# The mixture-of-experts phase: routing weights applied on VectorE, plain paced gathers, and row transpositions in the rounded type

## The chip, the cores and the metric

The kernel runs on one core of a Trainium2 chip. The metric is the device time of one execution in microseconds (us), as the median of several runs; lower is better.

## The reference, cut to what matters

Two decoder layers of attention, cross attention and a feed-forward network, each followed by a layer norm, over 16 x 128 tokens of width 512. The change touches the last network, in which each token goes to the two experts with the highest router scores (8 experts of inner width 352) and to a shared network:

```python
logits = x @ gate_weight.T
scores = jax.nn.softmax(logits, axis=-1)
topk_w, topk_idx = jax.lax.top_k(scores, 2)
combine = jnp.zeros((T, E), x.dtype).at[jnp.arange(T)[:, None], topk_idx].add(topk_w)
gu = jnp.einsum('th,efh->tef', x, gate_up_weights)
act = jax.nn.silu(gu[..., :F]) * gu[..., F:]
y = jnp.einsum('tef,te,ehf->th', act, combine, down_weights)
...
y = y + sact @ shared_down.T
...
x = _layernorm(x + y, axis=-1)
```

## The kernel before

Tokens lie in SBUF as `X`, 128 partitions by 16 token tiles by 512. The program is a row of phases. Each phase gives every engine its own stream of instructions with semaphores between them, written out by hand in the order in which they run. At a phase's end all engines meet at a barrier, clear the phase's semaphores (`Phase.__exit__`, ending at L175) and meet again; nothing of the next phase starts before the slowest engine is through.

Float32 products are made of three products in the rounded type (`float32r`, shown as fp32r): each operand is split into a rounded high part and the rest as a low part, and `products` (L97 to L99) adds high x high, high x low and low x high in PSUM. ScalarE (ACT) writes the high parts, VectorE (DVE) the low ones.

**The shared phase** (function around L1535 to L1900) computes the router, the two expert numbers of each token, their weights `S.score` (token tile t has its lower expert's weight in column t, the higher's in column 16 + t) and the slot of each (token, expert) pair in a list sorted by expert, `S.pos`. Every expert's stretch of slots is filled up to whole tiles of 128: 39 tiles (`TILES`). GpSimd (POOL) scatters the 16 token tiles to both slots in the DRAM tensor `x_slots` (L1624, 32 indirect DMAs), and then the weights to the slots of the DRAM tensor `s_slots`, one float for each partition (L1631, 32 indirect DMAs, a wait for all earlier ones ahead of every second, and a wait for all at the end). Meanwhile TensorE (PE) computes the shared network in loops, and DVE adds its rows to `X` (L1786).

**The expert phase** (`expert_ffn_phase`) runs over the 39 tiles. SP loads a tile of 128 rows of `x_slots` into one of four buffers `xin` (L1967) and its 128 weights into `sc` (L1970). PE transposes the rows in four 128 x 128 pieces (L2146; they are plain float32, against the identity `S.ident`), for tile i + 1 between the up products of tile i and the down products of tile i - 1. ACT and DVE split the result (L2050, L2086), PE makes gate and up (24 products' worth of 352 columns each in three parts), ACT and DVE apply silu and multiply (L2064, L2094), PE transposes the hidden rows (L2191, three pieces), and the down products follow. `store` on ACT copies the result out of PSUM and multiplies it by the row's weight `sc` (L2057); SP stores it to `y_slots` (L1983). POOL splits the next experts' weights (L2008, L2011) and loads the ones after.

**The end of the phase.** When every tile of the experts but the last is stored (`landed`, L2021), POOL issues 16 indirect gathers of the lower expert's rows that the DMA engines add onto `X` (L2035, `compute_op=ALU.add`), one for each token tile and none waiting for another. After the last tile's store has landed it issues 16 plain gathers of the higher expert's rows into `yg`, slices of the two weight staging buffers (L2038; shown as weights_raw and expert_raw). DVE adds each to `X` (L2118), takes the statistics of the row (L2121, L2124), POOL raises to the power -0.5 (L2029), ACT normalizes (L2077) and SP stores the output.

Of the kernel before, what the change touches and what calls it, by code (L numbers as in the profile page):

```python
# [11 lines left out]
P = 128  # L12
# [209 lines left out]
def attention_phase(nc, S, kind, w):  # L222
# [8 lines left out]
    with Phase(nc, kind) as phase:  # L231
# [175 lines left out]
        def _(sp):  # L407
# [30 lines left out]
            if kind == "decay":  # L438
                sp.wait_ge(zero_set, 1)
                with sp.Fori(0, SLOTS // P) as i:  # L440
                    for slots in (S.x_slots, S.y_slots):
                        rows = slots.rearrange("(i p) n -> i p n", p=P)[bass.ds(i, 1)].rearrange("o p n -> (o p) n")
                        sp.dma_start(rows, zeros[:, :]).then_inc(slots_zero, 16)
                sp.dma_start(S.s_slots.rearrange("(p i) n -> p (i n)", p=P), zeros[:, 0:TILES]).then_inc(slots_zero, 16)
                sp.wait_ge(slots_zero, 32 * (SLOTS // P) + 16)
                sp.dma_start(next_c, S.ctx_dram[:, 0:GT, :]).then_inc(next_c_in, 16)
                sp.wait_ge(pp_full, place[("v", G - 1, GT - 1)] + 1)
                sp.wait_ge(s_full, B - GT)
                sp.dma_start(next_q, S.cross["q"].rearrange("p c n -> p (c n)")).then_inc(next_q_in, 16)
                for i, n in enumerate("kv"):  # L450
                    sp.dma_start(next_kv[:, i, :], S.cross[n].rearrange("p c n -> p (c n)")).then_inc(next_kv_in, 16)
# [1065 lines left out]
def shared_ffn_phase(nc, S, w):  # L1517
# [13 lines left out]
    with Phase(nc, "shared") as phase:  # L1531
# [26 lines left out]
        slots_done, rows_done, scattered, scored = sem("slots_done"), sem("rows_done"), sem("scattered"), sem("scored")  # L1558
# [59 lines left out]
        @block.gpsimd  # L1618
        def _(pool):
            pool.wait_ge(slots_done, 1)  # L1620
            for t in range(B):
                for k in range(2):
                    at = bass.IndirectOffsetOnAxis(ap=S.pos[:, k * B + t:k * B + t + 1], axis=0)
                    pool.indirect_dma_start(S.x_slots, at, S.X[:, t, :], None).then_inc(scattered, 16)  # L1624
                if t % GT == GT - 1:
                    pool.wait_ge(scattered, 16 * 2 * (t + 1))
            for n in range(2 * B):
                at = bass.IndirectOffsetOnAxis(ap=S.pos[:, n:n + 1], axis=0)
                if n and n % 2 == 0:
                    pool.wait_ge(scored, 16 * n)  # L1630
                pool.indirect_dma_start(S.s_slots, at, S.score[:, n:n + 1], None).then_inc(scored, 16)  # L1631
            pool.wait_ge(scored, 16 * 2 * B)
# [283 lines left out]
def expert_ffn_phase(nc, S, w):  # L1916
# [8 lines left out]
    with Phase(nc, "expert") as phase:  # L1925
# [4 lines left out]
        xin = sb("xin", [P, NX, DM])  # L1930
# [5 lines left out]
        sc = sb("sc", [P, NX])  # L1936
# [9 lines left out]
        s_in = [sem(f"s_in{b}") for b in range(NX)]  # L1946
        low_added = [sem(f"low_added{b}") for b in range(B)]
        yg_in = [sem(f"yg_in{b}") for b in range(B)]
        high_added = sem("high_added")
        w_hi, w_ready, tile_done, spare_set = sem("w_hi"), sem("w_ready"), sem("tile_done"), sem("spare_set")  # L1950
        tr_full, tr_hi, tr_lo = sem("tr_full"), sem("tr_hi"), sem("tr_lo")
# [13 lines left out]
        def _(sp):  # L1965
            def load(i):
                sp.dma_start(xin[:, i % NX, :], rows(S.x_slots, i)).then_inc(x_in[i % NX], 16)  # L1967

            def load_score(i):
                sp.dma_start(sc[:, i % NX:i % NX + 1], rows(S.s_slots, i)).then_inc(s_in[i % NX], 16)  # L1970
# [3 lines left out]
            for i in range(NX):  # L1974
                load_score(i)
            for e in (1, 2):
                sp.dma_start(raw[e % 2][:, :], w["experts"][e * P:(e + 1) * P, :]).then_inc(first_in[e % 2], 16)
            for i in range(TILES):
# [5 lines left out]
                if i + NX < TILES:  # L1984
                    load_score(i + NX)
# [6 lines left out]
        def _(pool):  # L1992
# [41 lines left out]
            for t in range(B):  # L2034
                pool.indirect_dma_start(S.X[:, t, :], None, S.y_slots, slots(t), compute_op=ALU.add).then_inc(low_added[t], 16)  # L2035
            pool.wait_ge(y_out[(TILES - 1) % 2], 16 * ((TILES - 1) // 2 + 1))
            for t in range(B):
                pool.indirect_dma_start(yg[t], None, S.y_slots, slots(B + t)).then_inc(yg_in[t], 16)  # L2038
                if t >= 9 and t % 4 == 1:
                    norm(t // 4 - 2)  # L2040
# [4 lines left out]
        def _(act):  # L2045
# [6 lines left out]
            def store(i):  # L2052
# [3 lines left out]
                act.wait_ge(s_in[i % NX], 16 * (i // NX + 1))  # L2056
                act.activation(ys[:, i % 2, :], yb[i % 2], ACT.Copy, scale=sc[:, i % NX:i % NX + 1]).then_inc(y_copied, 1)  # L2057

            tokens(0)
# [21 lines left out]
        def _(dve):  # L2081
# [30 lines left out]

            ends = [hi - 1 for lo, hi in sets]
            for n in range(B + 2):
                if n < B:
                    dve.wait_ge(low_added[n], 16)
                    dve.wait_ge(yg_in[n], 16)
                    dve.tensor_tensor(S.X[:, n, :], S.X[:, n, :], yg[n], ALU.add).then_inc(high_added, 1)  # L2118
# [15 lines left out]
        def _(pe):  # L2134
# [5 lines left out]
            def transposes(i):  # L2140
                if i:
                    pe.wait_ge(x_in[i % NX], 16 * (i // NX + (i % NX > 0)))
                    pe.wait_ge(tr_lo, i)
                x = xin[:, i % NX, :] if i else S.first_x
                for c in range(C):
                    m = pe.transpose(tr[:, c * P:(c + 1) * P], x[:, c * P:(c + 1) * P], S.ident[:, :])  # L2146
# [51 lines left out]
def build(nc, a, out, phases=6):  # L2198

    with ExitStack() as ctx:  # L2200
# [19 lines left out]
        S.s_slots = nc.dram_tensor("s_slots", (SLOTS, 1), F32).ap()  # L2220
# [175 lines left out]
```

## Time and profile before

| | us |
|---|---|
| median of 3 runs | 2093.61 (2092.49 to 2094.29) |
| the profiled execution, its own time | 2087.5 |
| its span, first to last instruction | 2085.7 |
| PE busy | 1887.3 (90%) |
| DVE busy | 1041.1 (50%) |
| ACT busy | 713.2 (34%) |
| POOL busy | 385.6 (18%) |
| mean granted TensorE clock | 0.967 |

The span is what lies between the first and the last instruction; the execution's own time is 1.8 us longer. The median of the runs stands 6.1 us above the profiled execution. All positions in the trace (2011.69, say) are us from the start of the span. The granted clock is 1.00 at 2.4 GHz and 0.50 at 1.2 GHz.

### The profile page before, as it was taken

Reading aid. Unit: us, or ns where it says so; the run is one execution under the profiler, and the core shown is the slowest. Engines: PE = TensorE matmul, PEld = TensorE weight load, DVE = VectorE, ACT = ScalarE, POOL = GpSimd, SP = SyncE. Lnnn points to the kernel's source line nnn. Section 1 sums busy time; section 2 is a strip of 40 time slices with the busy share of each in tenths; the row PEclk is TensorE's granted clock in tenths of the full one; section 3 lists DMA queues with packets and bytes.
Section 4 is the critical chain, followed back from the end, with each engine's and each line's share of the span. In section 5 each row is a group of like instructions: output and inputs, shape, how many; then the busy total and the mean of one; then the engine's idle time right before and its main releaser. Section 6 shows DMA issues by size and latency. Waiting matters only on the chain. (4 is left out here: it accounts for less than half of the span.)

```text
span 2085.7 us, 32789 instructions
## 1 busy us (share of the span) xinstructions
PE 1887.3 (90%) x12124; PEld 1535.6 (74%) x12124; DVE 1041.1 (50%) x1836; ACT 713.2 (34%) x2275; POOL 385.6 (18%) x339
## 2 busy tenths in 40 slices
PE   8899888999999989999899998899879995999991
PEld 6667566788888767777677776677658874899990
DVE  5666753455555446333364547677865332222224
ACT  3555624334444332111231102545632210233332
POOL 1111100000000038000021100001104322745335
PEclk9999999999999999999999999999999998999995
DMA  7110142000000022000093000000015100644257
GB/s 238 42 46 14 43 160 82 1 1 1 1 1 1 1 76 91 1 0 0 24 352 115 1 20 27 26 2 1 2 46 207 46 0 0 243 149 143 82 114 205
DMA packets 73375, 135.89 MB, mean 65 GB/s; under 512 B 13456, under 2 KB 31760, under 8 KB 71184
## 3 DMA queue, kind: packets, MB, share of 16 engines
q1 hardware_dynamic: 47376, 96.28, 13.3%
q0 software_dynamic: 7888, 27.94, 4.5%
q10 hardware_dynamic: 17968, 9.71, 1.8%
q8 instruction: 96, 1.57, 0.3%
q14 instruction: 47, 0.39, 0.1%
HBM read 90.62 MB, written 43.29 MB: 64 GB/s over the span
## 5 line engine op out<-in xcount | busy, mean ns | idle before, releaser
L1473 PE MATMUL banks<-ternary_xth,ternary_wq 128*128 (+1 forms) x352 | 140.6, 399 | 5.0 <-DVE ternary_wq L1404 3.6
L1473 PE MATMUL banks<-ternary_xtl,ternary_wq 128*128 (+1 forms) x352 | 139.4, 396 | 0.0
L97 PE MATMUL banks<-latent_vh,latent_cth 128*128 128x512 f32 x256 | 104.2, 407 | 3.5 <-DVE latent_ctl L1174 3.5
L97 PE MATMUL banks<-weights,expert_xgh 128*128 x312 | 104.7, 336 | 2.4 <-DVE expert_xgl L2086 2.4
L99 PE MATMUL banks<-weights,expert_xgl 128*128 x312 | 101.6, 326 | 0.0
L573 ACT ACTIVATE gqa_pr<-banks,gqa_nb 128x128 f32<-128x128 f32 x256 | 90.4, 390 | 32.6 <-DVE gqa_nb L715 32.6
L98 PE MATMUL banks<-weights,expert_xgh 128*128 x312 | 101.4, 325 | 0.0
L573 ACT ACTIVATE causal_pr<-banks,causal_nb 128x128 f32<-128x128 f32 x256 | 90.4, 395 | 31.1 <-DVE causal_nb L715 31.1
L99 PE MATMUL banks<-latent_vh,latent_ctl 128*128 128x512 f32 x256 | 100.1, 391 | 0.0
L98 PE MATMUL banks<-latent_vl,latent_cth 128*128 128x512 f32 x256 | 100.1, 391 | 0.0
L1433 DVE TENSOR_TENSOR ternary_hf<-ternary_sg,banks 128x512 f32<-128x512 f32 x44 | 30.2, 687 | 135.4 <-issue 79.5
L1127 ACT ACTIVATE latent_pt<-banks 128x1024 f32<-128x1024 f32 x32 | 32.9, 1028 | 188.8 <-PE banks L1273 188.8
L1374 ACT ACTIVATE ternary_sg<-banks 128x512 f32<-128x512 f32 x44 | 26.4, 599 | 192.0 <-PE banks L1473 192.0
L1088 POOL TENSOR_TENSOR latent_rs<-latent_ve,mhalf 128x1 f32<-128x1 f32 x15 | 8.2, 550 | 445.6 <-DVE latent_ve L219 445.6
L1118 ACT ACTIVATE latent_pr<-banks,latent_nb 128x128 f32<-128x128 f32 x256 | 90.6, 374 | 0.0
L97 PE MATMUL banks<-latent_xgh,latent_ch 128*128 128x256 f32 x256 | 77.9, 304 | 9.4 <-DVE latent_xgl L1168 4.6
L1473 PEld LDWEIGHTS banks<-ternary_xth,ternary_wq 128*128 128x128 f32 x352 | 67.2, 191 | 23.2 <-DVE ternary_xtl L70 4.3
L1174 DVE TENSOR_TENSOR latent_ctl<-banks,latent_cth 128x512 fp32r<-128x512 f32 x64 | 42.9, 689 | 71.6 <-ACT latent_cth L1105 71.6
L1485 PE MATMUL banks<-ternary_wq,ternary_hh 128*128 128x512 f32 x176 | 70.8, 402 | 8.1 <-DVE ternary_hl L1437 5.8
L1473 PEld LDWEIGHTS banks<-ternary_xtl,ternary_wq 128*128 128x128 f32 x352 | 67.3, 191 | 14.2
L2094 DVE TENSOR_TENSOR expert_hf<-expert_sg,banks 128x352 f32<-128x352 f32 x39 | 20.4, 522 | 105.4 <-PE banks L99 102.9
L98 PE MATMUL banks<-latent_xgl,latent_ch 128*128 128x256 f32 x256 | 72.9, 285 | 0.0
(462 smaller groups left out, 5412.0 us busy)
## 6 DMA issues: line engine op xcount, KB each, us to landing
x_slots<-decay_zeros SPq DMA_DIRECT2D x39, 256.0 KB, 4.3
y_slots<-decay_zeros SPq DMA_DIRECT2D x39, 256.0 KB, 4.5
y_slots<-expert_ys SPq DMA_DIRECT2D x39, 256.0 KB
expert_xin<-x_slots SPq DMA_DIRECT2D x38, 256.0 KB, 2.9
weights_raw<-in_expert_experts SPq DMA_DIRECT2D x4, 2176.0 KB, 9.2
gqa_tw<-in_ternary_w ACTq DMA_DIRECT2D x4, 2112.0 KB
ternary_raw<-in_ternary_w SPq DMA_DIRECT2D x11, 768.0 KB, 4.1
expert_raw<-in_expert_experts POOLq DMA_DIRECT2D x3, 2176.0 KB, 9.7
```

Of the source, the lines that this page charges most:

```text
L97: pe.matmul(out, wh, xh, start=first, stop=False, **kw)
L98: pe.matmul(out, wh, xl, start=False, stop=False, **kw)
L99: return pe.matmul(out, wl, xh, start=False, stop=last, **kw)
L573: a = act.activation(pr[:, h, c, :], S.bank[2 * h + c // 4][:, (c % 4) * P:(c % 4 + 1) * P], ACT.Exp, bias=nb[:, h, c:c + 1], accum_out=su ...
L1118: a = act.activation(pr[:, c, :], S.bank[x][:, j * P:(j + 1) * P], ACT.Exp, bias=nb[:, c:c + 1], accum_out=sums[:, c:c + 1])
L1127: act.activation(pt[:, :, :], pair(1), ACT.Copy).then_inc(pt_done, 1)
L1174: dve.tensor_tensor(ctl[:, x, :], S.bank[2 + x], f32(cth[:, x, :]), ALU.subtract).then_inc(ct_lo, 1)
L1374: act.activation(sg[:, j % 2, :], gate[j % 2][:, :], ACT.Sigmoid).then_inc(sig_done, 1)
L1433: dve.tensor_tensor(hf[:, j % 2, :], sg[:, j % 2, :], up[j % 2][:, :], ALU.mult).then_inc(hf_done, 1)
L1473: a = pe.matmul(dst[:, :], wq[:, j, m, c * P:(c + 1) * P], x[:, c, toks], start=c == 0 and n == 0, stop=c == C - 1 and n == 1)
L1485: a = pe.matmul(yb[i][:, :], h[:, j % 2, i * P:(i + 1) * P], wq[:, j, 2, :], start=j == 0 and n == 0, stop=j == J - 1 and n == 1)
L2094: dve.tensor_tensor(hf[:, i % 2, :], sg[:, i % 2, :], up[i % 2][:, 0:F1], ALU.mult).then_inc(hf_done, 1)
```

## The change

Five things, all for the last network:

- The weights are not scattered to DRAM: the tensor `s_slots`, the DMA that filled it with zeros in an earlier phase, the 32 scatters, the 39 loads of `sc` and their semaphores go. `store` copies without a factor.
- The gathers of the lower expert's rows go into `yg` like the higher's, without an addition. Each from the third on waits until the one two before it has landed.
- DVE gets 16 instructions of a new kind behind its last tile: each multiplies a gathered row by its weight from `S.score` and adds `X`. Its 16 additions of the higher expert's rows become the same kind.
- The gather of the higher expert's rows for token tile t waits until DVE has used the lower rows in the same buffer (`low_added`).
- `xin` is declared in the rounded type, ACT makes a rounded identity `identr` at the phase's start, and the transpositions of tiles 1 to 38 take both and write PSUM in that type. Tile 0 keeps plain float32. The DMA still moves the same bytes into `xin`.

```diff
-                sp.dma_start(S.s_slots.rearrange("(p i) n -> p (i n)", p=P), zeros[:, 0:TILES]).then_inc(slots_zero, 16)
-                sp.wait_ge(slots_zero, 32 * (SLOTS // P) + 16)
+                sp.wait_ge(slots_zero, 32 * (SLOTS // P))
...
-            for n in range(2 * B):
-                at = bass.IndirectOffsetOnAxis(ap=S.pos[:, n:n + 1], axis=0)
-                if n and n % 2 == 0:
-                    pool.wait_ge(scored, 16 * n)
-                pool.indirect_dma_start(S.s_slots, at, S.score[:, n:n + 1], None).then_inc(scored, 16)
-            pool.wait_ge(scored, 16 * 2 * B)
...
-        xin = sb("xin", [P, NX, DM])
+        xin, identr = sb("xin", [P, NX, DM], F32R), sb("identr", [P, P], F32R)
...
-                sp.dma_start(xin[:, i % NX, :], rows(S.x_slots, i)).then_inc(x_in[i % NX], 16)
-
-            def load_score(i):
-                sp.dma_start(sc[:, i % NX:i % NX + 1], rows(S.s_slots, i)).then_inc(s_in[i % NX], 16)
+                sp.dma_start(f32(xin[:, i % NX, :]), rows(S.x_slots, i)).then_inc(x_in[i % NX], 16)
...
             for t in range(B):
-                pool.indirect_dma_start(S.X[:, t, :], None, S.y_slots, slots(t), compute_op=ALU.add).then_inc(low_added[t], 16)
+                if t >= 2:
+                    pool.wait_ge(low_in[t - 2], 16)
+                pool.indirect_dma_start(yg[t], None, S.y_slots, slots(t)).then_inc(low_in[t], 16)
             pool.wait_ge(y_out[(TILES - 1) % 2], 16 * ((TILES - 1) // 2 + 1))
             for t in range(B):
+                pool.wait_ge(low_added, t + 1)
                 pool.indirect_dma_start(yg[t], None, S.y_slots, slots(B + t)).then_inc(yg_in[t], 16)
...
-                act.wait_ge(s_in[i % NX], 16 * (i // NX + 1))
-                act.activation(ys[:, i % 2, :], yb[i % 2], ACT.Copy, scale=sc[:, i % NX:i % NX + 1]).then_inc(y_copied, 1)
+                act.activation(ys[:, i % 2, :], yb[i % 2], ACT.Copy).then_inc(y_copied, 1)
 
+            act.activation(identr[:, :], S.ident[:, :], ACT.Copy).then_inc(ident_rounded, 1)
...
+            def add_scored(n, k):
+
+                x = S.X[:, n, :]
+                return dve.scalar_tensor_tensor(out=x, in0=yg[n], scalar=S.score[:, k * B + n:k * B + n + 1], in1=x,
+                                                op0=ALU.mult, op1=ALU.add)
+
+            for n in range(B):
+                dve.wait_ge(low_in[n], 16)
+                add_scored(n, 0).then_inc(low_added, 1)
...
-                    dve.wait_ge(low_added[n], 16)
                     dve.wait_ge(yg_in[n], 16)
-                    dve.tensor_tensor(S.X[:, n, :], S.X[:, n, :], yg[n], ALU.add).then_inc(high_added, 1)
+                    add_scored(n, 1).then_inc(high_added, 1)
...
                 if i:
+                    pe.wait_ge(ident_rounded, 1)
                     pe.wait_ge(x_in[i % NX], 16 * (i // NX + (i % NX > 0)))
                     pe.wait_ge(tr_lo, i)
-                x = xin[:, i % NX, :] if i else S.first_x
                 for c in range(C):
-                    m = pe.transpose(tr[:, c * P:(c + 1) * P], x[:, c * P:(c + 1) * P], S.ident[:, :])
+                    cols = slice(c * P, (c + 1) * P)
+                    if i:
+                        m = pe.transpose(tr[:, cols].bitcast(F32R), xin[:, i % NX, cols], identr[:, :])
+                    else:
+                        m = pe.transpose(tr[:, cols], S.first_x[:, cols], S.ident[:, :])
```

How it moves instructions on POOL, at the end of the shared phase. Before, from the scatters of rows to the first instruction of the expert phase (L191 to L175 are the barrier and the clearing of the semaphores):

```order
L1624 DMA x_slots<-X,pos 4992x512 x32
L1631 DMA s_slots<-score,pos 4992x1 x32
L1913 UNCONDITIONAL_BRANCH
L191 UNCONDITIONAL_BRANCH
L194 ISA x6
L175 UNCONDITIONAL_BRANCH
L1991 UNCONDITIONAL_BRANCH
L1993 MEMSET expert_spare 128x1
```

With the change:

```order
L1623 DMA x_slots<-X,pos 4992x512 x32
L1906 UNCONDITIONAL_BRANCH
L191 UNCONDITIONAL_BRANCH
L194 ISA x6
L175 UNCONDITIONAL_BRANCH
L1976 UNCONDITIONAL_BRANCH
L1978 MEMSET expert_spare 128x1
```

The 32 scatters of weights were POOL's last work of the phase; now it goes from the scatters of rows straight to the barrier.

POOL at the end of the expert phase. Before:

```order
L2021 TENSOR_TENSOR expert_spare<-expert_spare 128x1
L2035 DMA X<-y_slots,pos 128x512 x16
L2038 DMA weights_raw<-y_slots,pos 128x512 x8
L2038 DMA expert_raw<-y_slots,pos 128x512 x2
L2029 TENSOR_TENSOR expert_rs<-expert_ve,mhalf 128x4
```

With the change:

```order
L2006 TENSOR_TENSOR expert_spare<-expert_spare 128x1
L2022 DMA weights_raw<-y_slots,pos 128x512 x8
L2022 DMA expert_raw<-y_slots,pos 128x512 x8
L2026 DMA weights_raw<-y_slots,pos 128x512 x8
L2026 DMA expert_raw<-y_slots,pos 128x512 x2
L2014 TENSOR_TENSOR expert_rs<-expert_ve,mhalf 128x4
```

The number of gathers is the same and so is their place behind `landed`; the first 16 now fill the buffers that the next 16 fill again.

## Rows read from the trace of the kernel before

**Rows 1.** The page, part 1: engine, busy us, share of the span, instructions.

```profile
PE 1887.3 (90%) x12124; PEld 1535.6 (74%) x12124; DVE 1041.1 (50%) x1836; ACT 713.2 (34%) x2275; POOL 385.6 (18%) x339
```

**Rows 2.** Timeline at this boundary: start us, us, engine, instruction, [idle before <-releaser].

```profile
1749.21 2.74 DVE L1786 TENSOR_TENSOR X<-X,banks 128x512 f32 x4 [1.17 <-PE banks L99]
...
1750.72 0.39 PE L99 MATMUL banks<-weights,shared_hl 64*128 64x512 f32 x1
...
1759.55 0.96 POOL L1631 DMA_INDIRECT s_slots<-score,pos  x1 [0.30 <-issue]
...
1771.95 0.10 POOL L1993 MEMSET expert_spare<- 128x1 f32 x1 [11.44 <-POOLq L175]
...
1771.99 1.09 PE L2146 MATMUL banks<-ident,first_x 128*128 128x128 f32 x4 [20.88 <-PEq L175]
```

**Rows 3.** Waits from 1650 us on: total us, times, longest.

```profile
POOL s_slots L1631 <- DMA s_slots<-score,pos: 78.0, 13, 7.4
```

**Rows 4.** Timeline at three other phase boundaries.

```profile
1530.99 0.55 DVE L624 TENSOR_SCALAR X<-X,causal_mv,causal_rs 128x512 f32<-128x512 f32 x1 [0.66 <-POOL causal_rs L483]
1533.47 2.79 PE L60 MATMUL banks<-ident,X 128*128 128x128 f32 x12 [5.12 <-PEq L175]
...
1037.40 1.94 PE L809 MATMUL banks<-ident,X 128*128 128x128 f32 x16 [2.81 <-PEq L175]
...
272.06 1.94 PE L1213 MATMUL banks<-ident,X 128*128 128x128 f32 x8 [2.76 <-PEq L175]
```

**Rows 5.** Stretches: us, busy PE, PEld, DVE, ACT, POOL, then granted clock, DMA share, GB/s.

```profile
1752.50:1753.00 0.50, 0.00 (x0) 0.00 (x0) 0.00 (x0) 0.00 (x0) 0.10 (x1) 0.91 0.00 0
...
1780.00:1781.00 1.00, 1.00 (x8) 1.00 (x7) 0.00 (x0) 0.00 (x0) 0.00 (x0) 0.89 0.85 366
...
272.00:274.00 2.00, 1.94 (x10) 1.98 (x10) 0.19 (x1) 0.60 (x1) 0.00 (x0) 0.50 0.42 91
...
1037.00:1039.00 2.00, 1.60 (x15) 1.63 (x16) 0.00 (x0) 0.00 (x0) 0.53 (x1) 1.00 0.29 90
```

**Rows 6.** The chain that ended last, expert phase: start us, us on it.

```profile
1778.57 0.29 PE banks L97
...
1784.09 0.16 PE banks L97
...
1887.72 0.44 PE banks L2146 x4
...
1894.39 0.44 PE banks L2146 x4
```

**Rows 7.** Groups by line and shape: busy us, mean ns of one.

```profile
L98 PEld LDWEIGHTS banks<-weights,expert_xgh 128*128 128x128 f32 x312 | 59.7, 191 | 0.0
...
L2146 PEld LDWEIGHTS banks<-ident,expert_xin 128*128 128x128 f32 x152 | 18.9, 140 | 0.8
...
L1404 DVE SCALAR_TENSOR_TENSOR ternary_wq<-ternary_raw,ternary_thr,ternary_below 128x512 fp32r<-128x512 f32 x33 | 25.7, 825 | 2.8 <-POOL ternary_below L1355 2.8
```

**Rows 8.** Timeline of the end of the expert phase.

```profile
2011.69 1.69 POOL L2035 DMA_INDIRECT X<-y_slots,pos  x1 [0.15 <-issue]
...
2037.97 0.56 DVE L2100 TENSOR_TENSOR expert_htl<-banks,expert_hth 128x384 fp32r<-128x384 f32 x1 [2.61 <-ACT expert_hth L2072]
...
2039.50 1.54 POOL L2035 DMA_INDIRECT X<-y_slots,pos  x1 [0.31 <-issue]
...
2042.00 0.69 ACT L2057 ACTIVATE expert_ys<-banks,expert_sc 128x512 f32<-128x512 f32 x1 [4.06 <-PE banks L99]
...
2046.16 0.99 POOL L2038 DMA_INDIRECT weights_raw<-y_slots,pos  x1 [5.12 <-DMA y_slots<-expert_ys]
...
2049.54 0.69 DVE L2118 TENSOR_TENSOR X<-X,weights_raw 128x512 f32<-128x512 f32 x1 [11.01 <-DMA weights_raw<-y_slots,pos]
```

**Rows 9.** DMA issues from 1650 us on: median us from issue to landing.

```profile
X<-y_slots,pos POOLq DMA_INDIRECT x16, 5.8
weights_raw<-y_slots,pos POOLq DMA_INDIRECT x8, 3.6
```

More of the change, by code:

```diff
@@ L1557, in shared_ffn_phase @@
         route_in, given_done, ranked = sem("route_in"), sem("given_done"), sem("ranked")
-        slots_done, rows_done, scattered, scored = sem("slots_done"), sem("rows_done"), sem("scattered"), sem("scored")
+        slots_done, rows_done, scattered = sem("slots_done"), sem("rows_done"), sem("scattered")
         gw_in, gw_zero, first_x_in = sem("gw_in"), sem("gw_zero"), sem("first_x_in")
@@ L1935, in expert_ffn_phase @@
         ys = sb("ys", [P, 2, DM])
-        sc = sb("sc", [P, NX])
         six, mv = sb("six", [P, B, 6]), sb("mv", [P, B, 2])
@@ L1945, in expert_ffn_phase @@
         y_out = [sem(f"y_out{b}") for b in range(2)]
-        s_in = [sem(f"s_in{b}") for b in range(NX)]
-        low_added = [sem(f"low_added{b}") for b in range(B)]
+        low_in = [sem(f"low_in{b}") for b in range(B)]
         yg_in = [sem(f"yg_in{b}") for b in range(B)]
-        high_added = sem("high_added")
+        low_added, high_added = sem("low_added"), sem("high_added")
         w_hi, w_ready, tile_done, spare_set = sem("w_hi"), sem("w_ready"), sem("tile_done"), sem("spare_set")
+        ident_rounded = sem("ident_rounded")
         tr_full, tr_hi, tr_lo = sem("tr_full"), sem("tr_hi"), sem("tr_lo")
@@ L1966, in load @@
             def load(i):
-                sp.dma_start(xin[:, i % NX, :], rows(S.x_slots, i)).then_inc(x_in[i % NX], 16)
-            def load_score(i):
-                sp.dma_start(sc[:, i % NX:i % NX + 1], rows(S.s_slots, i)).then_inc(s_in[i % NX], 16)
+                sp.dma_start(f32(xin[:, i % NX, :]), rows(S.x_slots, i)).then_inc(x_in[i % NX], 16)
             for i in range(1, NX):
                 load(i)
-            for i in range(NX):
-                load_score(i)
             for e in (1, 2):
@@ L1983, in _ @@
                 sp.dma_start(rows(S.y_slots, i), ys[:, i % 2, :]).then_inc(y_out[i % 2], 16)
-                if i + NX < TILES:
-                    load_score(i + NX)
             for t in range(B):
@@ L2219, in build @@
         S.landed_at = sb("landed_at", [P, E], U32)
-        S.s_slots = nc.dram_tensor("s_slots", (SLOTS, 1), F32).ap()
         S.ring, S.owner1 = sb("ring", [P, TILES], U32), sb("owner1", [P, TILES], U32)
```

## The prediction

> **What bounds the kernel now.** I read the busy shares first: PE works 90% of the span [rows 1], so only what PE executes, or what holds PE up, is worth much. The list of waits and the timeline around the start of the expert phase come next, since the change takes work out there. PE's last product before the barrier starts at 1750.72 and is over by 1751.11; DVE's last addition to `X` ends at 1749.21 + 2.74 = 1751.95; but the next phase starts only at 1771.95, after PE has stood idle for 20.88 us [rows 2]. POOL is what is late: its last scatter of weights is issued until 1759.55 + 0.96 = 1760.51 and then it waits 11.44 us for the landing and the barrier [rows 2]. It got so late because every second scatter waits for the ones before, 78.0 us over 13 waits, 6.0 us each [rows 3]. The third view is the chain that ended last, in the 39 tiles: it is PE's without a gap, a tile each 1894.39 - 1887.72 = 6.67 us, the four transpositions on it with 0.44 us [rows 6]. Of this stage only PE's own instructions count. The last view is the timeline behind the tiles: the store of the last tile (ACT at 2042.00, landed at 2046.16) and then POOL's 16 gathers, with DVE behind each [rows 8].
>
> **The change part by part.** The sum is made against the profiled execution's own 2087.5 us and then moved to the median of the runs, which stands 6.1 us higher (2093.6).
>
> (1) The 32 scatters of weights go. POOL's last work of the phase is then the scatters of rows, done long before, and DVE's addition that ends at 1751.95 becomes the last. What a barrier costs behind the last worker is shown by the boundary before: DVE ends at 1530.99 + 0.55 = 1531.54 and PE starts at 1533.47, 1.93 us [rows 4]. So the expert phase starts at 1751.95 + 1.93 = 1753.9 instead of 1772.0: **18.1 us**. All of it is on the path: PE waits from 1751.11 to the new phase and then runs without a gap. Next late would be DVE, whose addition waits for PE itself.
>
> (2) The clock after the shorter gap. Now PE restarts at the half clock: the four first transpositions take 1.09 us [rows 2] against 0.44, and 19 products take 0.29 us instead of 0.16 [rows 6] until the clock is back shortly after 1780 [rows 5]: 0.65 + 19 x 0.13 = 3.1 us lost. With the change PE is idle from 1751.11 to 1753.9, 2.8 us. Two earlier gaps of that length (2.81 and 2.76 us, [rows 4]) ended one at 1.00 and one at 0.50 [rows 5]. Here the clock had fallen by 1753 (0.91 over the half microsecond from 1752.50 [rows 5]), ahead of the new start, so the start is likely at the half clock again, with a return possibly sooner. Bounds 0 and 3.1; I take **1.0 us** gained.
>
> (3) The loads of weights and the zero fill. SP's 39 small loads go, of which the first four stand ahead of the two big weight loads. Nobody waits for those on PE: the chain in the tiles holds PE only. 0 us; covered by PE. The same for ACT's factor: a copy on ACT beside PE, 0 us apart from the last tile's. ACT's rounding of the identity stands ahead of its first copy, under the first transpositions: 0.
>
> (4) The transpositions of 38 tiles, 152 instructions, now cost 0.44 / 4 = 0.110 us each on the chain [rows 6]. No transposition and no product of under 256 columns in the rounded type is in the trace, so the new price is bounded. Below: a rounded product of 352 columns takes 0.16 us [rows 6], 147 ns of it at 2.4 columns a ns; 128 columns would be 53 ns, at most 14 ns more, and I take 53 as the end: 152 x 57 ns = 8.7 us gained. Above: the weight load of a rounded product takes 191 ns against 140 ns in a transposition [rows 7]; if the new form loads its weights the slow way, the 51 ns more stand where the stream saves, and nothing is gained, or it is even dearer (a rival below). The two rows pull apart equally and no row is nearer, so I take the middle, 85 ns: 152 x 25 ns = **3.8 us** gained, ends 0 and 8.7. The rule that speaks against this part: by the Trainium skill, "TensorE: Matmul & The Clock Gate", Terms (the row on the xbus), TRN2 has a transpose mode that is four times faster for float32. By that rule plain float32 rows already have the fast way and the retyping gives 0; that is the second rival below.
>
> (5) The gathers of the lower rows. Before, they start at 2011.69 and the last is issued until 2039.50 + 1.54 = 2041.04, 1.84 us apart [rows 8]; POOL then has 5.1 us of slack until the last store has landed at 2046.16. Now each is a plain gather, 0.99 us of issue, and two are in flight. A plain gather lands in 3.6 us, one with addition in 5.8 [rows 9]. With some 0.3 us to wake up, a pair takes 3.9 us, 1.95 each: 16 x 1.95 = 31.2 us, until 2042.9. That is still 3.3 us ahead of 2046.16, so 0 us; stores and row loads that run beside it may eat that margin, hence up to 2 us of loss in the range. The break-even is (2046.16 - 2011.69) / 16 = 2.15 us each.
>
> (6) DVE's new instructions. 16 multiply-adds begin once DVE has finished the last tile at 2037.97 + 0.56 = 2038.53 [rows 8]. The nearest price is an addition of the same size, 0.69 us [rows 8]; the only multiply-add of 512 columns in the trace takes 0.825 us [rows 7], with another output type. 16 x 0.69 = 11.0 us ends at 2049.6, when DVE is first wanted for a higher row (2049.54): hidden. By 0.825 it would end 2.2 us late and the 16 in the tail would each be 0.14 us longer, some 2 us in all. I take 0. POOL's added wait for `low_added` before each higher gather is met early: DVE works at 0.7 us a row from 2038.5, POOL issues at 1.3 us a row from 2046.
>
> (7) The last store. ACT's copy at 2042.00 starts 1 us after PE has ended and its buffer's previous store was still under way beside the adding gathers; the last store itself needs until 2046.16. With fewer transfers beside them I expect **1.0 us** less, bounds 0 and 1.6.
>
> Sum: 18.1 + 1.0 + 3.8 + 1.0 = 23.9 us. 2087.5 - 23.9 = 2063.6 for the profiled kind of execution, 2093.6 - 23.9 = **2069.7 us** for the median.
>
> **The rivals.**
>
> The retyping gives nothing: the rounded rows take 110 ns as before. For it speaks that the trace's transposition and plain product look alike and the slow weight load; against it the rounded stream. 2069.7 + 3.8 = 2073.5 us.
>
> The rounded type is dear when narrow: every rounded product here is at least 256 wide. If a 128-wide one went at the plain product's four passes, 4 x 53 = 213 ns, it would cost 152 x 103 ns = 15.7 us more than now: 2093.6 - 20.1 + 15.7 = 2089.2 us.
>
> The lower gathers are late because a gather beside the tiles' traffic takes 5.8 us, as the adding ones do now [rows 9]: a pair each 6.1 us, 16 x 3.05 = 48.8 us against the 34.5 there are, 14.3 us late: 2084.0 us. Against it: the adding ones read and write `X`, and the plain ones in the tail need 3.6 us.
>
> Slower than before: the same pacing, two at a time, makes the weights' scatters stand 6.0 us per pair in waits on top of 2.5 us of issue [rows 2, 3], 8.5 us a pair. If the lower gathers went like that, 16 x 4.25 = 68 us, the first higher gather would be 33.5 us late: 2103.2 us. It decides from 28 us of lateness on, (34.5 + 28) / 16 = 3.9 us a gather. Against it: those scatters write 4 bytes to each slot in DRAM, the gathers whole rows into SBUF.
>
> **How the numbers follow.** My forecast 0.48, the retyping gives nothing 0.29, dear when narrow 0.10, gathers at 5.8 us 0.09, gathers like the scatters 0.04. The forecast with all its ends spans 18.1 + 3.1 + 8.7 + 1.6 = 31.5 gained (2062) to 18.1 alone with 4 us lost in (5) and (6) (2079.5); that includes the first rival and leaves out the other three, some 0.2. A difference under 0.2% (4.2 us) can't be told from none here. Faster by more: the first two, gathers at 5.8 us, and half of the narrow case, whose 2089.2 lies at the bound (2089.4): 0.91. Within: 0.05. Slower: 0.04.
>
> **What would show it.** The gap of PE at the start of the expert phase shrinks from 20.9 to about 2.8 us and POOL has no indirect DMA behind the scatters of rows. The granted clock around the new start tells (2). The four transpositions on the chain take 0.34 us a tile if (4) holds, 0.44 if not, 0.85 if narrow is dear. POOL's lower gathers stand 1.8 to 2.1 us apart; if over 2.15, the first higher gather starts later than the last store's landing. DVE's multiply-adds show 0.69 or 0.83 us. The prediction is wrong if the gap stays above 5 us, or if the stretch from ACT's last copy to the end (43.7 us now, from 2042.00) grows.

## The result and the profile after

The median fell from 2093.12 us (2092.49 to 2094.29, 4 runs of each) to 2067.73 us (2067.34 to 2068.66): a ratio of 0.9881, 95% interval 0.9866 to 0.9897. The forecast was 2069.7 us, range 2062.0 to 2079.5. The profiled execution of the changed kernel took 2068.66 us, its span 2066.9 us.

The page of the changed kernel, part 1, answers to [rows 1]; POOL has 32 instructions and 39 us less:

```profile
PE 1886.0 (91%) x12124; PEld 1533.9 (74%) x12124; DVE 1052.3 (51%) x1852; ACT 708.4 (34%) x2276; POOL 346.9 (17%) x307
```

The timeline at the start of the expert phase, to be held against [rows 2]:

```profile
1749.13 2.76 DVE L1779 TENSOR_TENSOR X<-X,banks 128x512 f32 x4 [1.18 <-PE banks L99]
...
1750.66 0.39 PE L99 MATMUL banks<-weights,shared_hl 64*128 64x512 f32 x1
...
1753.09 0.10 POOL L1978 MEMSET expert_spare<- 128x1 f32 x1 [125.94 <-POOLq L175]
...
1753.13 1.09 PE L2147 MATMUL banks<-ident,first_x 128*128 128x128 f32 x4 [2.08 <-PEq L175]
```

POOL is now idle for 125.94 us until the expert phase starts, and PE stands for 2.08 us instead of 20.88. The tile loop on the chain that ended last, answering to [rows 6], with the products around the transpositions; first the changed kernel:

```profile
1866.73 0.16 PE banks L99
1866.89 0.30 PE banks L2145 x4
1867.19 0.30 PE banks L97
1867.49 0.23 PE banks L98
```

and the same place in the kernel before:

```profile
1887.56 0.16 PE banks L99
1887.72 0.44 PE banks L2146 x4
1888.15 0.23 PE banks L97
1888.39 0.23 PE banks L98
```

The four transpositions take 0.14 us less, and the first product behind them 0.07 us more. The timeline of the end, answering to [rows 8]:

```profile
1989.51 1.05 POOL L2022 DMA_INDIRECT weights_raw<-y_slots,pos  x1 [0.15 <-issue]
...
2016.06 5.38 DVE L2104 SCALAR_TENSOR_TENSOR X<-weights_raw,score,X 128x512 f32<-128x512 f32 x8
...
2018.66 0.60 ACT L2044 ACTIVATE expert_ys<-banks 128x512 f32<-128x512 f32 x1 [3.11 <-PE banks L99]
2019.51 1.42 POOL L2022 DMA_INDIRECT expert_raw<-y_slots,pos  x1 [0.57 <-DVE X L2104]
2021.36 5.38 DVE L2104 SCALAR_TENSOR_TENSOR X<-expert_raw,score,X 128x512 f32<-128x512 f32 x8
2022.39 5.17 POOL L2026 DMA_INDIRECT weights_raw<-y_slots,pos  x1 [1.46 <-DMA y_slots<-expert_ys]
2027.86 0.95 POOL L2026 DMA_INDIRECT weights_raw<-y_slots,pos  x1 [0.30 <-issue]
...
2029.94 0.75 DVE L2104 SCALAR_TENSOR_TENSOR X<-weights_raw,score,X 128x512 f32<-128x512 f32 x1 [3.20 <-DMA weights_raw<-y_slots,pos]
```

One row was not foreseen in the prediction: the first higher gather takes 5.17 us to issue, where it took 0.99 [rows 8]. In the same time DVE does its second eight multiply-adds.

So the span, 2085.7 to 2066.9 us, splits into four stretches without remainder:

| stretch | before | after | gained |
|---|---|---|---|
| span start to first transposition of the expert phase | 1771.99 | 1753.13 | 18.9 |
| from there to the end of PE's last product | 269.0 | 265.5 | 3.5 |
| from there to the first higher gather | 5.2 | 3.8 | 1.4 |
| first higher gather to the end | 39.5 | 44.5 | -5.0 |

The traces give 18.8 us, the medians 25.4 us. Of the 6.6 us between them, 5.6 are on the side of the kernel before, whose profiled execution lay that far under its median (2087.5 and 2093.12); the other 1.0 is the changed kernel's, whose profiled execution was its slowest (2068.66 against 2067.73). In the runs below, which stand beside 8 to 15 runs of the kernel before, that one has a median of 2082 to 2084 us, and the gain is 18.5 us. Why it stood near 2093 in the first measurement stays open.

### The profile page after: what moved, and what is told of

The parts are those of the page before. It is cut to its first block and busy times, and to the rows that moved or that the text cites. A ratio compares the mean times of both kernels' runs of the same rounds, so it can differ in the third digit from the quotient of the medians.

```text
span 2066.9 us, 32715 instructions
## 1 busy us (share of the span) xinstructions
PE 1886.0 (91%) x12124; PEld 1533.9 (74%) x12124; DVE 1052.3 (51%) x1852; ACT 708.4 (34%) x2276; POOL 346.9 (17%) x307
```

## The experiments

Positions in the table come from each run's profile: start of the expert phase (first transposition), the stretch of PE from there to the end of its last product, the issue time of the first higher gather, and the stretch from that gather to the end. The ratio is to runs of the kernel before that were timed beside it, with its 95% interval. The runs were made on four different chips, so across them only the ratios can be compared. The first group (r_before_again, r_round_only, r_after_again, r_plain_transposes) ran on one chip.

| run | median us | ratio | start | PE stretch | issue | to the end |
|---|---|---|---|---|---|---|
| r_before_again | 2084.16 (one) | | 1769.0 | 267.9 | 0.99 | 39.8 |
| r_no_scatter | 2064.91 | 0.9918 (0.9904 to 0.9932) | 1749.6 | 268.3 | 0.99 | 40.0 |
| r_round_only | 2082.37 | 0.9993 (0.9984 to 1.0002) | 1768.8 | 266.2 | 0.99 | 40.2 |
| r_after_again | 2065.21 | 0.9905 (0.989 to 0.992) | 1751.2 | 265.0 | 5.41 | 44.2 |
| r_plain_transposes | 2067.4 | 0.992 (0.9906 to 0.9933) | 1752.2 | 268.3 | 6.01 | 44.4 |
| r_low_narrow | 2059.69 | 0.9889 (0.987 to 0.9909) | 1751.1 | 265.2 | 0.95 | 39.5 |
| r_low_gap | 2062.72 | 0.9907 (0.9887 to 0.9926) | 1751.0 | 265.4 | 1.32 | 40.9 |
| r_low_split | 2063.01 | 0.9906 (0.9887 to 0.9925) | 1750.2 | 265.0 | 0.95 | 42.4 |
| r_gap_late | 2062.78 | 0.9908 (0.9893 to 0.9923) | 1752.8 | 265.3 | 0.96 | 40.1 |
| r_no_pace | 2080.28 | 0.9992 (0.9982 to 1.0002) | 1749.8 | 280.3 | 5.51 | 44.8 |
| r_pace4 | 2080.12 | 0.9994 (0.9984 to 1.0003) | 1750.5 | 280.4 | 5.49 | 44.4 |
| r_pace3 | 2067.26 | 0.9936 (0.9914 to 0.9959) | 1749.0 | 268.1 | 5.40 | 44.3 |

**Both kernels again.**

> The kernel before, unchanged, for a second trace of it. Theory A (the profiled execution of before was a quick one because its paced scatters of weights happened to land quickly): POOL's last scatter and so the start of the expert phase stand at another place, by 3 to 8 us later than 1772.0, with the row scatters, the tile period (6.67) and the tail as they were. Theory B (the 6 us between its time and the median lie anywhere else): the start of the expert phase is within 1 us of 1772.0.

> The changed kernel, unchanged, timed beside the others and traced a second time. Theory A (DVE's back-to-back multiply-adds hold off POOL's writing of the first higher gather until they are through): that gather's issue takes 4 to 6 us again and ends within 1 us of the end of the 16th multiply-add. Theory B (the 5.17 us were an accident of that execution): it takes 1.0 to 1.5 us and the tail from its start to the end is 40 us instead of 44.5.

For the kernel before neither theory holds: the expert phase starts at 1769.04, 3.0 us sooner than in the first trace, and not 3 to 8 us later or within 1 us. So the scatters had not landed unusually early in the first trace, and they don't explain the 6 us. For the changed kernel theory A holds: the issue takes 5.41 us and ends 0.83 us behind the 16th multiply-add.

The change is 18.5 us here by the medians (2083.74 of the 15 runs of the kernel before, 2065.21) and by the spans (2082.4, 2063.9). The parts are much the same as in the first pair: 17.9 at the start, 3.0 in PE's stretch, 2.1 ahead of the first higher gather, -4.4 behind it.

**The scatters alone taken out of the kernel before.** This run leaves out the routing weights, since nothing writes them to the slots.

```diff
-            for n in range(2 * B):
-                at = bass.IndirectOffsetOnAxis(ap=S.pos[:, n:n + 1], axis=0)
-                if n and n % 2 == 0:
-                    pool.wait_ge(scored, 16 * n)
-                pool.indirect_dma_start(S.s_slots, at, S.score[:, n:n + 1], None).then_inc(scored, 16)
-            pool.wait_ge(scored, 16 * 2 * B)
```

> The kernel before without its 32 scatters of the routing weights (it leaves out the weights: the tiles' factors are read as the zeros that the slots hold). All else as before, the 39 small loads of factors and the adding gathers too. Theory A (the scatters are the whole of the gain and the new end of the phase is a loss): the expert phase starts at about 1751 to 1753, 18 us earlier, the tail stays as before, and the kernel is 18 to 20 us faster than before, so as fast as the changed kernel with plain transpositions or up to 3 us faster. Theory B (the plain gathers bring a part of the gain): it is 2 us or more slower than that kernel.

Its median is 16.9 us under that of the kernel before, its span 19.2 us under r_before_again's, all of it at the start (1769.0 to 1749.6). The scatters by themselves make up the whole gain of the change as the repeated runs show it, within the intervals (0.9918 against r_after_again's 0.9905); the other four edits come to about nothing together. Only the first measurement, 0.9881 with its slow kernel before, lies outside. The next runs take that nothing apart.

**The rounded transpositions, alone and left out.** Once as the only edit to the kernel before (r_round_only), once the changed kernel without it (r_plain_transposes, whose edit this is):

```diff
                 for c in range(C):
                     cols = slice(c * P, (c + 1) * P)
-                    if i:
-                        m = pe.transpose(tr[:, cols].bitcast(F32R), xin[:, i % NX, cols], identr[:, :])
-                    else:
-                        m = pe.transpose(tr[:, cols], S.first_x[:, cols], S.ident[:, :])
+                    x = f32(xin[:, i % NX, cols]) if i else S.first_x[:, cols]
+                    m = pe.transpose(tr[:, cols], x, S.ident[:, :])
```

> The kernel before with nothing but the rounded transpositions. Theory A: 2.4 us faster than before, tile period 6.61, the gap ahead of the expert phase unchanged at some 20 us. Theory B: 5.6 us faster. Theory C: no change.

> The changed kernel with its 152 row transpositions in plain float32 against the plain identity. Theory A (the trace's reading: a rounded transposition is 37 ns shorter, but the product behind it grows from 0.23 to 0.30 us because its weight load is no longer covered, so the retyping gives 0.06 us a tile): 2.4 us slower than the changed kernel, tile period 6.67. Theory B (the retyping is worth its full 0.15 us a tile): 5.6 us slower than the changed kernel. Theory C (worth nothing): the same time as the changed kernel within 0.7 us.

ACT's silu, one in each tile, shows the period without PE's modelled ends. From the timelines of ACT, two tiles that lie 26 apart, in r_plain_transposes:

```profile
1798.43 0.46 ACT L2052 ACTIVATE expert_sg<-banks 128x352 f32<-128x352 f32 x1 [1.28 <-PE banks L99]
...
1972.28 0.46 ACT L2052 ACTIVATE expert_sg<-banks 128x352 f32<-128x352 f32 x1 [1.28 <-PE banks L99]
```

and in r_after_again:

```profile
1803.43 0.47 ACT L2052 ACTIVATE expert_sg<-banks 128x352 f32<-128x352 f32 x1 [0.70 <-PE banks L99]
...
1975.12 0.47 ACT L2052 ACTIVATE expert_sg<-banks 128x352 f32<-128x352 f32 x1 [1.27 <-PE banks L99]
```

173.85 / 26 = 6.687 us against 171.69 / 26 = 6.603 us: 0.08 us a tile, 38 x 0.08 = 3.0 us. In the kernel before the same two places give 6.683, in r_round_only 6.603. PE's stretch agrees in sign: 3.3 us shorter with the rounded form in the changed kernel, 1.8 us in the kernel before. In the latter pair the clock adds its own share: it was back 5.75 us after the start in r_before_again and 8.75 us in r_round_only. The medians (2.2 us between the two changed ones, 0.9993 for the edit alone) agree, but couldn't have told it from nothing.

**DVE's multiply-adds beside POOL's first higher gather.** Three ways to take DVE out of POOL's way. r_low_narrow cuts the lower multiply-adds to 2 of 512 columns and so leaves most of the lower expert's rows out of the sum:

```diff
-            def add_scored(n, k):
+            def add_scored(n, k, w=DM):
...
-                x = S.X[:, n, :]
-                return dve.scalar_tensor_tensor(out=x, in0=yg[n],
+                x = S.X[:, n, 0:w]
+                return dve.scalar_tensor_tensor(out=x, in0=yg[n][:, 0:w],
...
-                add_scored(n, 0).then_inc(low_added, 1)
+                add_scored(n, 0, 2).then_inc(low_added, 1)
```

> The changed kernel with the 16 multiply-adds of the lower rows cut to 2 of 512 columns (it leaves out nearly all of the lower expert's contribution). Theory A (they hold off POOL's first higher gather and delay the tail): that gather's issue takes about 1 us, the tail from its start to the end is 39.5 to 41 us instead of 44.5, 3 to 5 us faster than the changed kernel. Theory B (the tail is longer for another reason, the dearer multiply-adds of the higher rows or the transfers): the tail stays at 43 us or more and the time within 1.5 us of the changed kernel.

r_low_gap keeps them whole, but each waits until the one before is finished, which leaves a pause between them; r_low_split does eight ahead of the higher rows and each of the other eight behind a higher one. The edit of r_low_gap:

```diff
             for n in range(B):
                 dve.wait_ge(low_in[n], 16)
+                if n:
+                    dve.wait_ge(low_added, n)
                 add_scored(n, 0).then_inc(low_added, 1)
```

> The changed kernel, where each lower multiply-add waits for the one before it to be finished, which leaves a pause of some 0.1 us between them. Theory A1 (POOL is held off because DVE's instructions overlap without a pause): the first higher gather's issue takes under 2 us, the tail is 2 to 4 us shorter. Theory A2 (each multiply-add holds POOL off by itself, pauses that short don't let it in): issue again until DVE is through, which is now 1.5 to 2 us later, and the time is 1 to 2 us longer than the changed kernel's.

> The changed kernel with the lower multiply-adds of token tiles 8 to 15 moved behind the higher ones of tiles 0 to 7, so that DVE rests when the first higher gathers are issued. Theory A: the first gather's issue takes about 1 us and the first higher row is added 4 us earlier; but DVE then carries 2.1 us of work for each of the first 8 rows, more than the 1.45 us between gathers, so the net is between 0 and 3 us faster than the changed kernel. Theory B (POOL isn't held off by DVE): issue unchanged at 5 us, time the same or 2 to 4 us longer.

The timeline of POOL in r_low_narrow:

```profile
2020.74 0.95 POOL L2026 DMA_INDIRECT weights_raw<-y_slots,pos  x1 [3.66 <-DMA y_slots<-expert_ys]
2021.99 0.95 POOL L2026 DMA_INDIRECT weights_raw<-y_slots,pos  x1 [0.31 <-issue]
```

and of POOL and DVE in r_low_gap:

```profile
2013.91 6.73 DVE L2104 SCALAR_TENSOR_TENSOR X<-weights_raw,score,X 128x512 f32<-128x512 f32 x8
...
2020.15 1.32 POOL L2026 DMA_INDIRECT weights_raw<-y_slots,pos  x1 [2.10 <-DMA y_slots<-expert_ys]
...
2020.75 6.74 DVE L2104 SCALAR_TENSOR_TENSOR X<-expert_raw,score,X 128x512 f32<-128x512 f32 x8
2021.77 1.41 POOL L2026 DMA_INDIRECT weights_raw<-y_slots,pos  x1 [0.30 <-DVE X L2104]
```

With DVE nearly idle the issue is back at 0.95 us and the end at 39.5 us, the value of before. With the same arithmetic and a pause, 0.84 instead of 0.67 us apart (6.73 / 8 and 5.38 / 8), the issue takes 1.32 us. So it is DVE's uninterrupted row of multiply-adds that holds POOL's issue, not the landing of the store or a semaphore: the semaphore that this gather waits for, the first of `low_added`, had come over 5 us before in the first profile. In all six profiles with the unbroken row, the held issue ends 0.82 to 0.83 us behind DVE's last multiply-add: 2022.39 + 5.17 = 2027.56 behind 2021.36 + 5.38 = 2026.74 in the first profile. The traces of the kernel before have the same hold, without any multiply-add. One of the scatters that the change removes is issued while DVE makes the low parts of a block of weights in one long subtraction, from two operands in SBUF. From the timeline of the kernel before:

```profile
1664.31 4.69 DVE L1685 TENSOR_TENSOR weights<-weights_raw,weights 128x4352 fp32r<-128x4352 f32 x1 [6.00 <-ACT weights L1650]
1665.46 4.38 POOL L1631 DMA_INDIRECT s_slots<-score,pos  x1 [5.82 <-DMA s_slots<-score,pos]
```

Most other scatters take 0.96 us to issue. This one ends at 1669.84, 0.84 us behind DVE's 1669.00; in r_before_again it is 4.43 us and 0.82 us, in r_round_only 5.41 and 0.83. So the hold is not peculiar to the multiply-adds, and it could be seen before the change.

But each cure costs part of what it gives: with the pause the row ends later (2027.49) and delays the first higher additions, and the split moves eight of them, 0.67 us each, into the tail, where DVE then sets the pace (42.4 us to the end).

r_gap_late puts the pause only behind the tenth:

```diff
+                if n >= 10:
+                    dve.wait_ge(low_added, n)
                 add_scored(n, 0).then_inc(low_added, 1)
```

> The changed kernel, where the lower multiply-adds from the eleventh on wait for the one before. Theory A (only DVE's back-to-back work beside the first higher gathers' issues matters, and DVE's total work limits the rest): first gather's issue under 1.5 us, lower multiply-adds through about 1.5 us sooner than with a pause after each, and 1 to 2 us faster than that kernel, 3 to 4.5 us faster than the changed one. Theory B (the pauses cost nothing or help elsewhere): the same time as with a pause after each.

The issue takes 0.96 us, as theory A has it, but the ratio is that of r_low_gap, as theory B has it. The three forms with whole rows lie at 0.9906 to 0.9908, r_after_again at 0.9905, r_low_narrow at 0.9889 with an interval that overlaps it; the whole forms win 2 to 4 us between the first higher gather and the end, but no faster kernel than the change is shown. What shows the hold is the traces, not the times.

**How many lower gathers are in flight.** Any number, four or three instead of two. The edit of the first, r_no_pace:

```diff
             for t in range(B):
-                if t >= 2:
-                    pool.wait_ge(low_in[t - 2], 16)
                 pool.indirect_dma_start(yg[t], None, S.y_slots, slots(t)).then_inc(low_in[t], 16)
```

> The changed kernel without the waits between the lower gathers. Theory A (what matters there is only DVE, which starts on them after its last tile anyway): lower gathers issued 1.25 us apart and over by 2010, the time within 1 us of the changed kernel's. Theory B (16 gathers in flight crowd the queues that the tiles' stores and loads use): stores of the last tiles take 1 us or more longer, the time 1 to 3 us longer. Theory C (the paced gathers end too late and hold up the higher ones): 1 to 2 us faster.

> The changed kernel with four lower gathers in flight where it has two. Theory A (a tile's store waits in the queues behind all the gathers in flight, so the cost grows only with a backlog): a store takes 2 to 3 us longer than beside two, the buffer of the next copy is still free in time, and the time is the changed kernel's within 1.5 us. Theory B (any backlog beyond two stalls the tiles): PE waits 3 us or more among the last tiles, 3 to 10 us slower than the changed kernel.

> The changed kernel with three lower gathers in flight instead of two (each waits for the third before it). It tells where between two in flight (PE undisturbed, its last product at 2015.8 to 2018.6 us, 2065.2 us in all) and four in flight (PE without work for some 14 us, last product at 2030.4, 2080.1 us in all) the loss sets in. Theory A, the loss grows with the gathers' share of the DMA engines: three in flight lie between, a median of 2068 to 2075 us and a wait of ACT for something remote of 3 to 8 us. Theory B, it is a tipping point, in which one transfer that the tiles need gets through or not: either as with two, 2062 to 2067 us and no such wait, or as with four, 2079 to 2081 us and a wait of 13 to 14 us. I take B, and as with four the likelier of its two.

Here the surprise is large. Unpaced and with four in flight, the kernel is as slow as before the change (0.9992 and 0.9994), 15 us slower than with two, where no theory set down before these two had more than 10. Stretches of r_pace4: us, busy PE, PEld, DVE, ACT, POOL, granted clock, DMA share, GB/s:

```profile
1995.00:2000.00 5.00, 3.97 (x23) 3.29 (x22) 0.56 (x1) 0.49 (x1) 3.63 (x5) 1.00 0.80 255
2000.00:2005.00 5.00, 0.71 (x2) 0.19 (x1) 0.00 (x0) 0.00 (x0) 3.78 (x5) 0.78 0.72 206
2005.00:2010.00 5.00, 0.00 (x0) 0.00 (x0) 0.00 (x0) 0.12 (x1) 1.68 (x2) 0.50 0.58 170
```

Its waits from 1995 to 2012 us:

```profile
ACT expert_sg L2052 <- remote: 13.7, 1, 13.7
DVE expert_hf L2082 <- ACT expert_sg L2052: 13.7, 1, 13.7
...
DVE expert_htl L2088 <- issue: 4.4, 1, 4.4
```

And the timeline of the same stretch:

```profile
1996.57 0.46 PE L2145 MATMUL banks<-expert_identr,expert_xin 128*128 128x128 f32 x4
...
1999.21 0.19 PEld L98 LDWEIGHTS banks<-weights,expert_hth 96*128 96x128 f32 x1 [0.89 <-issue]
1999.93 0.39 PE L98 MATMUL banks<-weights,expert_hth 96*128 x1 [1.03 <-issue]
...
2001.34 0.39 PE L99 MATMUL banks<-weights,expert_htl 96*128 x1 [1.01 <-issue]
...
2006.03 0.95 POOL L2022 DMA_INDIRECT expert_raw<-y_slots,pos  x1 [0.30 <-issue]
2009.88 0.46 ACT L2052 ACTIVATE expert_sg<-banks 128x352 f32<-128x352 f32 x1 [13.75 <-remote]
2010.24 0.59 ACT L2038 ACTIVATE expert_xgh<-banks 128x512 fp32r<-128x512 f32 x1
```

ACT's silu at 2009.88 needs the gate product of its tile, which PE makes ahead of the up product and of the transpositions at 1996.57, and a buffer that DVE had long freed. No wait for a DMA stands in ACT's stream ahead of it. PE shows pauses of about 1 us in the same time that the profile ascribes to nothing ("issue"). The other idle times are no stalls of their own: DVE's 4.4 us ("issue") end at 1996.17 as ACT's copy of the hidden rows does (1995.64 + 0.49 = 1996.13), DVE then waits 13.65 us for ACT's silu, and PE 9.2 us for DVE behind it. ACT goes on at 2009.88, when the gathers are through: the queue of the gathers fills 71.7% of the DMA engines' time from 2008 to 2009, and 3.3% from 2009 to 2010. r_no_pace shows the same place of ACT:

```profile
2009.22 0.46 ACT L2050 ACTIVATE expert_sg<-banks 128x352 f32<-128x352 f32 x1 [13.70 <-remote]
```

Its last lower gather was issued until 2006.20, against 2006.98 in r_pace4, so ACT goes on 2.9 to 3.0 us behind the last issue in both. With three in flight the same kind of wait is there, but shorter (3.8, 1.5 and 3.2 us, "remote", for ACT), and PE's stretch is 3 us longer than with two; with two there is none. I had taken theory B for three, and the waits speak for A; the median, 2067.26 us, lies between the two, and the ratio's interval (0.9914 to 0.9959) overlaps that of two in flight. So three cost some 3 us in one trace, and four as much as all sixteen, 15 us.

What the engines lack in this time isn't shown. That it is their instructions, which come by DMA too, is my guess: the pauses hit engines whose inputs were in place, and the profile's instruction queue, which brings a packet every 14 to 18 us in the runs with two in flight (here within 1988 to 1990 us), has the next within 2016 to 2018 us only. Against it speaks that ACT goes on at 2009.88, more than 6 us ahead of that packet, and in r_no_pace at 2009.22 with the packet behind 2016. An experiment that separates it was not made. Nor was it tried to put the hidden rows' transpositions into the rounded type, or to place multiply-adds between the last tiles.

## Why the prediction was right, step by step

The predicted time holds, 2.0 us from the median, and the cause of the gain is the one named, the scatters. That the sum comes so close is luck. It has one wrong term, (6), and by the traces 23.9 us were forecast and 18.8 came. The median of the kernel before stood near 2093 in that measurement, for no reason that the runs show, and so the gain by medians was 25.4 us; in the repeated runs it is 18.5, 5.4 us less than forecast.

(1) The scatters. Forecast 18.1, measured 18.9. The addition of DVE was last, as said; the barrier behind it cost 1.2 us (1751.89 to 1753.13) instead of the 1.93 from another boundary. In the second pair it is 17.9. r_no_scatter shows the term by itself.

(2) The clock. Forecast 1.0, measured 3.5 - 38 x 0.067 = 1.0 us in the first pair (the first kernel pair's tile period went from 6.683 to 6.617). In the second pair it is 0: r_plain_transposes and r_no_scatter start early and have PE stretches of 268.3 against 267.9 us. PE restarts at half clock either way, as forecast. Read in steps of 0.25 us, with the short gap the granted clock rises 6.25 to 6.5 us after the start in all eleven profiles. With the long gap it rises after 8.0, 5.75 and 8.75 us (the first trace, r_before_again, r_round_only). So the 1.0 us is gained against two of the three, and nothing against the third; what decides between them isn't shown. The stretches of the changed kernel, answering to [rows 5]:

```profile
1752.50:1753.00 0.50, 0.00 (x0) 0.00 (x0) 0.00 (x0) 0.00 (x0) 0.00 (x0) 0.70 0.00 0
1753.00:1758.00 5.00, 3.26 (x11) 2.89 (x12) 0.69 (x1) 0.91 (x2) 0.17 (x3) 0.50 0.71 262
1758.00:1760.00 2.00, 2.00 (x9) 2.00 (x9) 0.00 (x0) 0.28 (x1) 0.00 (x0) 0.62 0.99 409
1760.00:1762.00 2.00, 1.96 (x15) 1.80 (x13) 0.22 (x1) 0.19 (x2) 0.00 (x0) 1.00 1.04 444
```

(3) The small loads, the copy without a factor and the rounding of the identity: nothing of them is on the path, as said. ACT's rounding of the identity, 0.31 us, lies under the first transpositions.

(4) The transpositions. Forecast 3.8 from 85 ns each; measured 2.5 to 3.0. The direction was right and the single one gains more than forecast, 0.30 / 4 = 75 ns, a saving of 35 ns and not 25; their weight load takes 141 ns as before, not the 191 of a rounded product. What I didn't look at is the product behind them, which gives back 0.07 of the 0.14 us. The two errors partly cancel. The rival that retyping gives 0 (the first in the list, though (4) of the prediction calls it the second) doesn't hold on the chain here: 0.44 us became 0.30. I had drawn it from the Trainium skill, "TensorE: Matmul & The Clock Gate", Terms, which states a transpose mode four times faster for float32; whether the plain rows run in it no run here shows.

(5) The lower gathers. Forecast 1.95 us each, measured (2019.51 - 1989.51) / 15 = 2.00 us, and the last is issued 1.46 us ahead of the last store's landing: 0 on the path, as forecast. What I held for a cost, the wait of each gather for the one two before, turned out to be what keeps the tiles going; without it the change gives nothing at all (0.9992). I had weighed only how late the gathers get, and not what they do to the tiles beside them.

(6) The multiply-adds: this is the step that failed. "Hidden", I wrote, since DVE would be done when the first higher row is wanted, and for POOL's wait I counted only the semaphore. The row of 16 takes 10.7 us, 0.67 us apart, as priced, but it holds off POOL's first higher gather by 4.2 us (5.17 instead of 0.99). The stretch behind the first higher gather's start lost 5.0 us in the first pair and 4.4 in the second, where the hold alone is 4.4 (5.41 instead of 0.99); the other 0.8 us of the first pair are open. The dearer multiply-adds of the tail (0.75 us against 0.69 for an addition) are not what costs: r_low_narrow keeps them and its stretch is 39.5 us, 4.7 less than r_after_again's and as before the change. A row of the kernel before would have warned: the scatter at 1665.46, whose issue took 4.38 us under a long DVE instruction. The prediction's own sign for being wrong, a longer stretch behind ACT's last copy, appeared: 2066.9 - 2018.66 = 48.2 us against 43.7.

(7) The last store. Forecast 1.0, bounds 0 to 1.6, measured 1.4 in the first pair and 2.1, above the bounds, in the second: ACT's copy starts 0.03 us after PE's end and the store lands 3.1 us behind the copy in the first profile.

The rivals: rounded rows that gain nothing or are dear, and gathers at 5.8 us or like the scatters, are all refuted by the rows above; the lower gathers beside the tiles land in 3.4 to 4.0 us (medians by buffer, three profiles). None of the rivals, and neither end of the range, had the hold of POOL or the starving of the tiles in it.

## What to carry to other kernels

Small scatters at a phase's end that wait for each other are worth removing where all engines meet behind them: the gain was the whole idle time of PE there, less the barrier. When a gather moves beside a running matmul stage, limit how many are in flight and look at the stage's engines, not at the gather; two were harmless here, three cost some 3 us in one trace, and four gave back the whole gain. And when work is put on VectorE "because it is idle", look at what GpSimd has to issue in that time, since an engine can be held without any semaphore between the two. One issue of 4.38 us among others of 0.96 in the trace of before is worth a look before the sum is made.

## What the runs showed of the hardware that was not expected

- An unbroken row of VectorE multiply-adds (128 x 512, float32, two operands from SBUF) held the issue of an indirect gather on GpSimd for 5.2 to 6.0 us, until 0.8 us after its end; with 0.17 us more between them the issue took 1.3 us. One long VectorE subtraction (128 x 4352, 4.69 us) held the issue of an indirect scatter in the same way for 4.4 to 5.4 us, in three profiles of kernels with the scatters. The hold isn't total: the last lower gathers, issued under the first eight multiply-adds of the row, took 0.94 to 1.43 us. What tells these from the first higher gather is open.
- With four indirect gathers of 256 KB in flight, and with all sixteen, ScalarE stood for 13.7 us with its inputs in place, VectorE waited behind it, and so did TensorE after pauses of its own of about 1 us; with three ScalarE stood for 3.8 us at most, with two not at all.
- The rounded transposition of 128 x 128 takes 75 ns against 110 ns in float32, but the next product takes 0.30 us instead of 0.23, so that four in a row win some 0.07 to 0.08 us and not 0.14.
